# Four neighbouring tokens in a partition: another order of tokens inside a chunk of 512

## The chip, the cores and the metric

The kernel runs on one core of a Trainium2 chip. The metric is the device time of one execution in microseconds; the time of a version is the median over its runs. The trace was recorded by the hardware profiler in one further execution.

## What is computed

The reference is a two-layer network over x of shape (8, 128, 16, 16): 8 images, 128 channels, 256 places, so 2048 tokens of 128 channels. Each layer adds an attention block and then a mixture of experts to x. Cut to what matters here:

```python
x = x + _L0_conv_ref(_ln_c(x), ...)                   # linear attention with 5x5 depthwise convolutions
t = _to_tokens(x)                                     # (8, 256, 128)
t = t + _L0_ffn_ref(_ln_t(t), gate_w, w1, b1, w2, b2) # 8 experts, the best 2 of each token, gelu
x = _from_tokens(t, x)
x = x + _L1_conv_ref(_ln_c(x), wq, ..., bo)           # softmax attention over the 256 places of an image
t = _to_tokens(x)
t = t + _L1_ffn_ref(_ln_t(t), router_w, gate_w, up_w, down_w)  # 16 experts, the best 2, silu(gate) * up
```

In both mixtures a token's two best experts by router logit are taken, a softmax over those two logits gives their weights, and the token gets the weighted sum of the two experts' outputs.

## The kernel before

x lies in SBUF as `xs`, 128 channels in the partitions and 2048 tokens along the row, in 4 chunks of 512 tokens (`CH = 512`, `NCH = 4`). Five engines each run a program of their own; the order on each is written out by hand, and semaphores join them. SP and ACT each issue DMAs on a queue of their own, and POOL issues the indirect ones.

A mixture of experts (r = 0 and r = 1) runs in these steps:

1. **Rows.** `token_rows` on TensorE multiplies, for each of 16 tiles of 128 tokens, the tile of `xs` (the stationary operand) by a matrix that removes the mean over channels and gives the router logits. The result has tokens in the partitions. ScalarE scales it (L665) into `ln_sq`, and SP stores the rows, one DMA for a chunk, to `tok_dram[r]` in DRAM (`rows_store`, L395). Tile t of a chunk holds its tokens 128t to 128t + 127, one in each partition, so the store moves runs of 512 bytes.
2. **Router.** `router` on VectorE picks two experts for each token and works out, with TensorE's `slots`, a place for each of the 4096 pairs (token, choice) in a list ordered by expert. `pair_id` holds the number of the token that stands in each partition and tile, and from it come the lists `token` and `dest` (L969, L970).
3. **Gathers.** POOL fetches 32 blocks of 128 rows from `tok_dram` by `token` (L510), after all four stores have landed and `token` is ready.
4. **Experts.** For 39 (r = 0) or 47 (r = 1) items TensorE turns a block, multiplies it by the expert's weights (L1342, L1359), with ScalarE and VectorE in between; the sums go to `y_acc`.
5. **Scatters.** POOL writes the 32 blocks of outputs to `y_dram[r]` by `dest` (L517): first choices in the upper 2048 rows, second choices in the lower.
6. **Loaded back.** `y_load` waits until all scatters have landed and then issues four DMAs of 256 KB on SP's queue (first choices, into `xc`) and four on ACT's queue (second choices, into `ln_sq`), L364, each again in runs of 512 bytes. Chunk c is ready when both of its DMAs have landed (`y_in[c]`).
7. **Sum.** For each of 16 tiles ScalarE weighs the first choice (L711, `weigh_first`) and VectorE adds the weighed second one (L1056, `moe_sum`). After the four tiles of a chunk TensorE turns them into one PSUM bank (L1369, `y_columns`), and VectorE adds the bank to the chunk of `xs` (L1060). On VectorE the four adds of chunk c stand ahead of the L1060 of chunk c - 1.

What follows the sum of r = 0 is the layer norm of the second layer: TensorE's L1122 of chunk c - 1 stands behind the turns of chunk c, and its L1127 behind all of these. What follows the sum of r = 1 is the store of each chunk to `out` (L435).

Of the kernel before, what the change touches and what calls it, by code (L numbers as in the profile page):

```python
# [34 lines left out]
ALU = mybir.AluOpType  # L35
# [3 lines left out]
C = 128  # L39
B, HW = 8, 16  # L40
S = HW * HW
T = B * S
CH = 512
NCH = T // CH
TT = T // 128
# [21 lines left out]
E0, F0 = 8, 512  # L67
E1, F1 = 16, 256
# [37 lines left out]
def metaformer(nc, x, x_tok, qkv_w, taps_in, late_w, w1, w2, b2, up1, down1, out):  # L106


    tok_dram = [nc.dram_tensor(f"tok{r}", (T, C), F32, kind="Internal").ap() for r in range(2)]
# [3 lines left out]
    with ctx:  # L113
        def sb(name, shape, dt=F32, own=ctx):
            return own.enter_context(nc.sbuf_tensor(name, shape, dt))

        def sem(name):
            return ctx.enter_context(nc.semaphore(name))

        bank = [ctx.enter_context(nc.psum_tensor(f"bank{i}", [128, CH], F32)) for i in range(8)]  # L120
# [11 lines left out]
        pair_id = sb("pair_id", [128, 2, TT], F16)  # L132
        tok_w = sb("tok_w", [128, 2, C + E1])
# [21 lines left out]
        xs = sb("xs", [128, T])  # L155
# [117 lines left out]
        y_in = [sem(f"y_in{c}") for c in range(NCH)]  # L273
# [31 lines left out]
        def conv_send(queue, u, i, part=0, parts=1):  # L305

            t, v = UNITS[u]
            n = G8 // parts
            a = G8 * (v * GU + i) + n * part
            queue.dma_start(heads_agg[t][a:a + n, :, :, :].rearrange("p x y b -> p x (y b)"),  # L310
                            conv_out[n * part * HW:n * (part + 1) * HW, u % 2, i, :]).then_inc(conv_sent[u % 2], 16)
# [37 lines left out]
        def row_tile(r, i):  # L349

            n = C + (E0, E1)[r]
            return bank[ROW_BANKS[r][i // 3]][:, (i % 3) * n:(i % 3 + 1) * n]
# [3 lines left out]
        def chunk(t, c, n=CH):  # L356
            return t[:, c * n:(c + 1) * n]


        def y_load(queue, r, k):  # L360

            queue.wait_ge(moe[r].scattered, 16 * NB)
            for c in range(NCH):
                queue.dma_start(chunk((xc, ln_sq)[k], c).rearrange("p (t c) -> p t c", c=C),  # L364
                                y_dram[r][k * T + c * CH:k * T + (c + 1) * CH, :]
                                .rearrange("(t p) c -> p t c", p=128)).then_inc(y_in[c], 16)

        @block.sync
        def _(sp):
            def x_load(c):  # L370

                sp.dma_start(chunk(xs, c), chunk(x, c)).then_inc(x_in[c], 16)

            def xt_load(c):

                sp.dma_start(chunk(xc, c), chunk(x_tok, c)).then_inc(xt_in[c], 16)

            xt_load(0)
            xt_load(1)
            x_load(0)  # L380
            xt_load(2)
            x_load(1)
            xt_load(3)
            x_load(2)
            x_load(3)
            for i, (a, b) in enumerate(TAP_PARTS):
                sp.dma_start(taps[:, a:b, :], taps_in[:, a:b, :]).then_inc(taps_landed[i], 16)
                if i == 2:
                    sp.dma_start(wT[:, W_P0:W_SM + 1, :], late_w).then_inc(w_in, 16)

            def rows_store(r):

                for c in range(NCH):
                    sp.wait_ge(rows_copied, TT * r + 4 * c + 4)
                    sp.dma_start(tok_dram[r][c * CH:(c + 1) * CH, :].rearrange("(t p) c -> p t c", p=128),  # L395
                                 chunk(ln_sq, c).rearrange("p (t c) -> p t c", c=C)).then_inc(rows_out[r], 16)

            for n in range(len(UNITS) + MAPS_AHEAD):
                if n < len(UNITS):
                    t, v = UNITS[n]  # L400
                    sp.wait_ge(head_a, NCH * (n // UPT + 1))
                    for g in range(v * GU, (v + 1) * GU):
                        sp.dma_start(cmap[:, t, g, :],
                                     heads_raw[t][G8 * g:G8 * (g + 1), :, :, :].rearrange("p x y b -> p x (y b)"))\
                            .then_inc(map_in[n], 16)
                if n >= MAPS_AHEAD:
                    u = n - MAPS_AHEAD
                    if u < LAST:
                        sp.wait_ge(conv_copied, u + 1)
                        for i in (1, 3):  # L410
                            conv_send(sp, u, i)
            for i in range(GU):
                sp.wait_ge(conv_copied, LAST + 1 + i)
                conv_send(sp, LAST, i, 0, 2 if i == GU - 1 else 1)
            sp.wait_ge(conv_mm, LAST + GU)
            for i in range(2):
                sp.wait_ge(conv_sent[i], CONV_SENT[i])
            sp.dma_start(w_up0[:, :], w1).then_inc(moe_w[0], 16)
            sp.dma_start(w_down0[:, :], w2).then_inc(moe_w[0], 16)
            sp.wait_ge(x1_ready, NCH)  # L420
            sp.dma_start(b2_all[:, :], b2.rearrange("(a e) f -> a (e f)", a=1).broadcast_to([128, E0 * C]))\
                .then_inc(moe_w[0], 16)
            rows_store(0)

            for i in range(W1_LOADS):
                sp.wait_ge(moe[0].turned, 4 * i + 4)
                for w, src, n in ((w_up1, up1, 2 * F1), (w_down1, down1, 2 * C)):
                    cols = slice(i * E1 // W1_LOADS * n, (i + 1) * E1 // W1_LOADS * n)
                    sp.dma_start(w[:, cols], src[:, cols]).then_inc(moe_w[1], 16)
            y_load(sp, 0, 0)  # L430
            rows_store(1)
            y_load(sp, 1, 0)
            for c in range(NCH):
                sp.wait_ge(x_moe, NCH + c + 1)
                sp.dma_start(chunk(out, c), chunk(xs, c)).then_inc(stored, 16)  # L435
            sp.wait_ge(stored, 16 * NCH)
# [4 lines left out]
        def _(pool):  # L441
# [29 lines left out]
            def table(out, pattern, base, step):  # L471
                pool.iota(out, pattern, base=base, channel_multiplier=step,
                          allow_small_or_imprecise_dtypes=True).then_inc(tables, 1)
            table(low_high[:, 0, :], [[0, 2 * TT]], 127, 0)
            table(low_high[:, 1, :], [[0, 2 * TT]], (NB - 1) * 128, 0)
            table(pair_id[:, 0, :], [[128, TT]], 0, 1)
            table(pair_id[:, 1, :], [[128, TT]], -T, 1)
            table(col_id[:, :], [[0, 1]], 0, 1)
            table(item_id[:, :], [[1, NI1]], 0, 0)
            pool.memset(ones16[:, :], 1.0).then_inc(tables, 1)  # L480
# [276 lines left out]
        def _(dve):  # L757
# [118 lines left out]
            for n in range(B + 6):  # L876
                if n >= 7 and n % 2 == 1:
                    c = (n - 7) // 2
# [170 lines left out]
            def moe_sum(r):  # L1049

                dve.wait_ge(rt_weights, r + 1)
                for c in range(NCH + 1):
                    for i in range(4 * c, min(4 * c + 4, TT)):
                        rows = slice(i * 128, (i + 1) * 128)
                        dve.wait_ge(y_weighed, TT * r + i + 1)
                        dve.scalar_tensor_tensor(out=xc[:, rows], in0=ln_sq[:, rows], scalar=pair_w[:, 1, i:i + 1],  # L1056
                                                 in1=xc[:, rows], op0=ALU.mult, op1=ALU.add).then_inc(y_added, 1)
                    if c >= 1:
                        dve.wait_ge(y_turned, NCH * r + c)
                        dve.tensor_tensor(chunk(xs, c - 1), chunk(xs, c - 1), bank[c - 1][:, :], ALU.add)\  # L1060
                            .then_inc(x_moe, 1)

            router(0, E0)
# [9 lines left out]
            for i in range(B + 6):  # L1073
# [20 lines left out]
                if i >= 7 and i % 2 == 1:  # L1094
                    c = (i - 7) // 2
# [10 lines left out]
        def _(pe):  # L1106
# [114 lines left out]
            for s in range(GU * len(UNITS)):  # L1221
# [18 lines left out]
                u, i = s // GU, s % GU  # L1240
                t, v = UNITS[u]
# [8 lines left out]
                for k in (2, 1, 3, 0, 4):  # L1250
                    y0, y1 = max(0, EDGE - k), min(HW, HW + EDGE - k)
                    mm = pe.matmul(bank[b][:, i * 128 + y0 * B:i * 128 + y1 * B], cw[:, u % CWR, i, k, :],  # L1252
                                   cmap[:, t, v * GU + i, (y0 + k - EDGE) * B:(y1 + k - EDGE) * B],
                                   start=(k == EDGE), stop=(k == 4))
# [10 lines left out]
            def token_rows(r, g):  # L1265

                pe.wait_ge((x1_ready, x3_ready)[r], ROW_GROUPS[g][-1] // 4 + 1)
                for i in ROW_GROUPS[g]:
                    mm = pe.matmul(row_tile(r, i), xs[:, i * 128:(i + 1) * 128], tok_w[:, r, 0:C + (E0, E1)[r]],  # L1269
                                   start=True, stop=True)  # L1270
                mm.then_inc(rows_mm, 1)

            pe.wait_ge(router_out, 3)
            for n in range(B + 4):
# [6 lines left out]
                if n >= 5 and n % 2 == 1:  # L1281
                    c = (n - 5) // 2
# [104 lines left out]
            for g in range(4):  # L1387
                for j in range(4):
                    i = 4 * g + j
                    mm = pe.matmul(bank[V_BANKS[g]][:, j * 128:(j + 1) * 128], xn[:, i * 128:(i + 1) * 128],  # L1390
                                   wT[:, W_AV, :], start=True, stop=True)
# [36 lines left out]
            for i in range(B + 5):  # L1428
# [6 lines left out]
                if i >= 6 and i % 2 == 0:  # L1435
                    c = (i - 6) // 2
# [70 lines left out]
```

## Time and profile before

| what | value |
|---|---|
| median of 3 runs | 446.07 us (444.70 to 447.37) |
| the profiled execution's own time | 447.75 us |
| its span, first to last instruction | 446.0 us |
| PE busy / weight loads / DVE / ACT / POOL | 79% / 68% / 50% / 47% / 40% of the span |
| mean granted clock of TensorE | 0.892 of full speed |
| DMA | 38.47 MB in 34184 packets, 28640 of them under 2 KB |

The busy shares are means over stages with different limits. TensorE is busiest, and over the whole span the chain that ended last lies 63% on PE, 8% on DMA and 8% on DVE. Between the last scatter and the last sum of each layer TensorE has nothing to do but the turns, so those two stretches, some 13 us each, are read by themselves.

### The profile page before, as it was taken

Reading aid. Unit: us, or ns where it says so; the run is one execution under the profiler, and the core shown is the slowest. Engines: PE = TensorE matmul, PEld = TensorE weight load, DVE = VectorE, ACT = ScalarE, POOL = GpSimd, SP = SyncE. Lnnn points to the kernel's source line nnn. Section 1 sums busy time; section 2 is a strip of 40 time slices with the busy share of each in tenths; the row PEclk is TensorE's granted clock in tenths of the full one; section 3 lists DMA queues with packets and bytes.
Section 4 is the critical chain, followed back from the end, with each engine's and each line's share of the span. In section 5 each row is a group of like instructions: output and inputs, shape, how many; then the busy total and the mean of one; then the engine's idle time right before and its main releaser. Section 6 shows DMA issues by size and latency. Waiting matters only on the chain.

```text
span 446.0 us, 7931 instructions
## 1 busy us (share of the span) xinstructions
PE 352.9 (79%) x2404; PEld 301.4 (68%) x2404; DVE 222.9 (50%) x565; ACT 210.9 (47%) x554; POOL 178.0 (40%) x202
## 2 busy tenths in 40 slices
PE   3889999997956598957999399898267988977813
PEld 1359999985734598957998265776246888877802
DVE  3618555513675156534776373776841343444306
ACT  4651333333574256734663364566533565554304
POOL 3819554400033655573556000003066555555530
PEclk9999999999896679995999789999665999999875
DMA  7444444324822546310111700000311111111146
GB/s 239 202 74 99 102 96 83 48 37 70 343 73 88 194 176 239 124 49 30 37 38 43 194 2 0 1 1 0 96 42 41 43 43 37 44 36 37 35 119 194
DMA packets 34184, 38.47 MB, mean 86 GB/s; under 512 B 3680, under 2 KB 28640, under 8 KB 33376
## 3 DMA queue, kind: packets, MB, share of 16 engines
q1 hardware_dynamic: 22620, 25.79, 19.8%
q0 software_dynamic: 4096, 8.40, 6.0%
q10 hardware_dynamic: 7428, 3.77, 3.9%
q8 instruction: 22, 0.36, 0.3%
q14 instruction: 18, 0.15, 0.1%
HBM read 24.31 MB, written 7.34 MB: 71 GB/s over the span
## 4 chain that ended last, share of the span: by engine, by line
PE 63%; DMA 8%; DVE 8%; ACT 6%; issue 6%; another core or an unknown queue 5%; ACTq 1%; POOL 1%; SPq 1%; POOLq 0%; DVEq 0%
PE bank L1342 18%; PE bank L1359 12%; PE bank L1252 10%; DMA ln_sq<-y 2%; PE bank L1204 2%; PE bank L1351 2%; PE bank L1424 2%; PE bank L1269 2%; PE bank L1189 2%; ACT w_block L684 2%; PE bank L1383 2%; POOL y L517 1%; PE bank L1133 1%; DMA x_rows<-tok,token 1%
## 5 line engine op out<-in xcount | busy, mean ns | idle before, releaser
L1342 PE MATMUL bank<-x_cols,w_block 128*128 x688 | 104.0, 300 | 20.5 <-ACT w_block L684 9.7
L1342 PEld LDWEIGHTS bank<-x_cols,w_block 128*128 128x128 f32 x688 | 94.1, 212 | 24.5 <-issue 24.3
L510 POOL DMA_INDIRECT x_rows<-tok,token x64 | 60.6, 947 | 65.2 <-DVE dest L970 26.9
L517 POOL DMA_INDIRECT y<-wide,dest x64 | 62.1, 970 | 49.4 <-DVE wide L1046 39.6
L1359 PE MATMUL bank<-w_down,h_cols 128*128 x500 | 75.4, 290 | 4.8 <-DVE wide L1046 3.2
L1359 PEld LDWEIGHTS bank<-w_down,h_cols 128*128 128x128 f32 x500 | 66.9, 203 | 7.3 <-issue 7.0
L1252 PE MATMUL bank<-cmap,cw 128*128 128x112 f32 (+2 forms) x480 | 57.4, 275 | 1.9 <-DMA cmap<-heads 1.9
L1252 PEld LDWEIGHTS bank<-cmap,cw 128*128 128x128 f32 x480 | 55.7, 192 | 3.7 <-DMA cmap<-heads 2.7
L684 ACT ACTIVATE w_block<-w_up 128x512 f32 x86 | 53.6, 623 | 0.9 <-issue 0.9
L321 POOL TENSOR_TENSOR cw<-taps 128x640 f32<-128x640 f32 x24 | 35.7, 1514 | 36.7 <-PE bank L1252 29.5
L1029 DVE TENSOR_TENSOR h_cols<-h_in,bank 128x256 f32<-128x256 f32 x47 | 19.8, 421 | 53.4 <-ACT h_in L701 32.0
L504 POOL MEMSET wide<- 128x4096 f32 x2 | 7.0, 3512 | 98.3 <-DVE xs L1097 60.7
L687 ACT ACTIVATE x_cols<-bank 128x128 f32<-128x128 f32 x64 | 16.3, 275 | 50.8 <-PE bank L1351 29.6
L1021 DVE TENSOR_TENSOR h_in<-bank,wT 128x512 f32<-128x512 f32 x39 | 26.9, 691 | 24.2 <-remote 13.0
L695 ACT ACTIVATE h_cols<-h_in 128x512 f32<-128x512 f32 x39 | 24.5, 629 | 22.7 <-DVE h_in L1021 19.3
L701 ACT ACTIVATE h_in<-bank 128x256 f32<-128x256 f32 x47 | 17.9, 383 | 20.2 <-PE bank L1342 16.7
L1351 PE MATMUL bank<-ident,x_rows 128*128 128x128 f32 x64 | 18.1, 308 | 9.5 <-ACT x_cols L687 5.1
L321 DVE TENSOR_TENSOR cw<-taps 128x640 f32<-128x640 f32 x24 | 23.7, 1020 | 2.2 <-PE bank L1252 2.2
L1369 PE MATMUL bank<-ident,wide 128*128 128x128 f32 x32 | 8.1, 403 | 19.8 <-DVE wide L1056 19.8
L711 ACT ACTIVATE wide<-wide,pair_w 128x128 f32<-128x128 f32 x32 | 10.2, 390 | 26.2 <-DMA ln_sq<-y 26.2
L1369 PEld LDWEIGHTS bank<-ident,wide 128*128 128x128 f32 x32 | 5.6, 205 | 24.1 <-DVE wide L1056 23.2
L1046 DVE SCALAR_TENSOR_TENSOR wide<-bank,item,wide 128x128 f32 x47 | 16.3, 347 | 8.2 <-PE bank L1359 6.6
(188 smaller groups left out, 524.8 us busy)
## 6 DMA issues: line engine op xcount, KB each, us to landing
w_up<-in_up_dram SPq DMA_DIRECT2D x4, 1024.0 KB
cmap<-heads SPq DMA_DIRECT2D x48, 64.0 KB
w_up<-in_w_dram SPq DMA_DIRECT2D x1, 2048.0 KB, 7.7
w_down<-in_w_dram SPq DMA_DIRECT2D x1, 2048.0 KB, 13.7
tok<-ln_sq SPq DMA_DIRECT2D x8, 256.0 KB, 2.4
w_down<-in_down_dram SPq DMA_DIRECT2D x4, 512.0 KB
wide<-y SPq DMA_DIRECT2D x8, 256.0 KB, 5.6
ln_sq<-y ACTq DMA_DIRECT2D x8, 256.0 KB, 6.1
```

The costliest lines, as they stand in the source:

```text
L321: engine.tensor_tensor(cw[:, u % CWR, i, :, :].rearrange("p k (o x) -> p k o x", x=HW), taps[:, g, KS * HW:TAP].unsqueeze(1).unsqueeze(3). ...
L510: pool.indirect_dma_start(out=x_rows[:, j % RING, :], out_offset=None, in_=tok_dram[r], in_offset=bass.IndirectOffsetOnAxis(ap=token[r][:, ...
L517: pool.indirect_dma_start(out=y_dram[r], in_=y_acc[:, s * C:(s + 1) * C], in_offset=None, out_offset=bass.IndirectOffsetOnAxis(ap=dest[r][ ...
L684: act.activation(w_block[:, n % 3, :], (w_up0, w_up1)[r][:, bass.ds(e * F0, F0)], ACT.Copy).then_inc(m.w, 1)
L695: act.activation(h_cols[:, j % HBUF, :], h_in[:, j % HBUF, :], ACT.Gelu_apprx_tanh)\
L701: act.activation(h_in[:, j % HBUF, 0:F1], bank[2 + j % UPS][:, 0:F1], ACT.Silu)\
L1021: dve.tensor_tensor(h_in[:, j % HBUF, :].rearrange("p (k s) -> p k s", k=M0), bank[2 + j % UPS][:, :].rearrange("p (k s) -> p k s", k=M0), ...
L1029: dve.tensor_tensor(h_cols[:, j % HBUF, 0:F1], h_in[:, j % HBUF, 0:F1], bank[2 + j % UPS][:, F1:2 * F1], ALU.mult).then_inc(m.h_in, 1)
L1252: mm = pe.matmul(bank[b][:, i * 128 + y0 * B:i * 128 + y1 * B], cw[:, u % CWR, i, k, :], cmap[:, t, v * GU + i, (y0 + k - EDGE) * B:(y1 + ...
L1342: mm = pe.matmul(bank[2 + j % UPS][:, i * 128:(i + 1) * 128], w_block[:, j % 3, i * 128:(i + 1) * 128], x_cols[:, bass.ds(place[j] & ((NB ...
L1351: pe.transpose(bank[k % 2][:, 0:128], x_rows[:, k % RING, :], ident[:, :]).then_inc(m.turned, 1)
L1359: mm = pe.matmul(bank[6 + j % 2][:, 0:C], h_cols[:, j % HBUF, i * 128:(i + 1) * 128], w_down[:, bass.ds(ej * (K * C) + i * C, C)], start=( ...
```

## The change

Inside a chunk, partition p now holds tokens 4p to 4p + 3 of the chunk, and tile j of the chunk holds the tokens 4p + j. Five places follow from this:

- `rows_store` and `y_load` describe the DRAM side as `(p t)` in place of `(t p)`: a partition's four rows are neighbours in DRAM, one run of 2 KB.
- `pair_id` is filled by the new numbering (two iota instructions, as before, of another pattern).
- `token_rows` takes the stationary operand through `tokens_of`: every fourth token of a chunk, a step of 16 bytes in place of neighbouring words.
- The L1060 add reads the turned bank in the order of the tokens: four words 512 bytes apart, then the next four. Its other operand and its output stay contiguous.

Counts and sizes of instructions, of DMAs and of their bytes stay the same. Which rows of a block stand in which order changes.

```diff
+        def tokens_of(t, i):
+            return chunk(t, i // 4).rearrange("p (q j) -> p j q", j=4)[:, i % 4, :]
...
                 queue.dma_start(chunk((xc, ln_sq)[k], c).rearrange("p (t c) -> p t c", c=C),
                                 y_dram[r][k * T + c * CH:k * T + (c + 1) * CH, :]
-                                .rearrange("(t p) c -> p t c", p=128)).then_inc(y_in[c], 16)
+                                .rearrange("(p t) c -> p t c", p=128)).then_inc(y_in[c], 16)
...
-                    sp.dma_start(tok_dram[r][c * CH:(c + 1) * CH, :].rearrange("(t p) c -> p t c", p=128),
+                    sp.dma_start(tok_dram[r][c * CH:(c + 1) * CH, :].rearrange("(p t) c -> p t c", p=128),
                                  chunk(ln_sq, c).rearrange("p (t c) -> p t c", c=C)).then_inc(rows_out[r], 16)
...
-            table(pair_id[:, 0, :], [[128, TT]], 0, 1)
-            table(pair_id[:, 1, :], [[128, TT]], -T, 1)
+            table(pair_id[:, 0, :].rearrange("p (c j) -> p c j", c=NCH), [[CH, NCH], [1, 4]], 0, 4)
+            table(pair_id[:, 1, :].rearrange("p (c j) -> p c j", c=NCH), [[CH, NCH], [1, 4]], -T, 4)
...
-                        dve.tensor_tensor(chunk(xs, c - 1), chunk(xs, c - 1), bank[c - 1][:, :], ALU.add)\
+                        xs_c = chunk(xs, c - 1).rearrange("p (q j) -> p q j", j=4)
+                        dve.tensor_tensor(xs_c, xs_c, bank[c - 1][:, :].rearrange("p (j q) -> p q j", j=4), ALU.add)\
                             .then_inc(x_moe, 1)
...
-                    mm = pe.matmul(row_tile(r, i), xs[:, i * 128:(i + 1) * 128], tok_w[:, r, 0:C + (E0, E1)[r]],
+                    mm = pe.matmul(row_tile(r, i), tokens_of(xs, i), tok_w[:, r, 0:C + (E0, E1)[r]],
                                    start=True, stop=True)
```

## Rows read from the trace of the kernel before

**Rows 1.** The chain that ended last, r = 0: start, length, what
```profile
139.34 2.50 DMA x_rows<-tok,token
...
247.54 5.57 DMA ln_sq<-y
...
254.84 1.12 PE bank L1369 x4
...
259.16 0.44 PE bank L1369 x4
```

**Rows 2.** The same chain, sum of r = 1
```profile
436.08 0.41 ACT wide L711
...
437.75 0.60 DVE xs L1060
438.35 1.20 DVE wide L1056 x4
...
441.33 1.13 PE bank L1369 x4
...
442.49 0.69 DVE xs L1060
```

**Rows 3.** Timeline of both sums: start, length, engine, line [idle before, releaser]
```profile
247.05 2.14 ACTq L364 DMA_DIRECT2D ln_sq<-y  x4
251.38 1.28 ACT L711 ACTIVATE wide<-wide,pair_w 128x128 f32<-128x128 f32 x4 [11.01 <-DMA ln_sq<-y]
...
258.33 0.69 DVE L1060 TENSOR_TENSOR xs<-xs,bank 128x512 f32<-128x512 f32 x1
...
430.15 2.13 ACTq L364 DMA_DIRECT2D ln_sq<-y  x4
434.33 1.28 ACT L711 ACTIVATE wide<-wide,pair_w 128x128 f32<-128x128 f32 x4 [12.25 <-DMA ln_sq<-y]
434.83 1.16 DVE L1056 SCALAR_TENSOR_TENSOR wide<-ln_sq,pair_w,wide 128x128 f32<-128x128 f32 x4 [9.05 <-ACT wide L711]
...
436.52 1.23 DVE L1056 SCALAR_TENSOR_TENSOR wide<-ln_sq,pair_w,wide 128x128 f32<-128x128 f32 x4 [0.53 <-ACT wide L711]
```

**Rows 4.** Timeline and DMA issues of the rows' store
```profile
131.72 3.45 SPq L395 DMA_DIRECT2D tok<-ln_sq  x4
...
tok<-ln_sq SPq DMA_DIRECT2D x8, 256.0 KB, 2.4
```

**Rows 5.** Windows; the last two columns are DMA share and GB/s
```profile
250.50:255.50 5.00, 1.77 (x7) 1.37 (x8) 3.10 (x10) 3.12 (x10) 0.00 (x0) 0.56 1.16 291
...
7.00:8.00 1.00, 0.00 (x0) 0.00 (x0) 0.27 (x3) 0.76 (x3) 0.00 (x0) 1.00 1.03 387
...
7.00:9.50 2.50, 0.41 (x1) 0.41 (x2) 1.59 (x12) 2.01 (x8) 0.00 (x0) 1.00 0.97 327
```

**Rows 6.** Timeline of the start, and DMA issues: KB each, us to landing
```profile
0.80 0.87 SPq L376 DMA_DIRECT2D wide<-in_x_tok_dram  x2
4.91 0.87 DVE L785 BATCH_NORM_STATS2 x_stat<-wide 128x6 f32<-128x128 f32 x4 [4.91 <-DMA wide<-in_x_tok_dram]
...
b_all<-in_b_dram SPq DMA_DIRECT2D x1, 512.0 KB, 3.6
```

**Rows 7.** Groups by line and shape: busy us, mean ns | idle before
```profile
L1060 DVE TENSOR_TENSOR xs<-xs,bank 128x512 f32<-128x512 f32 x8 | 5.5, 683 | 1.2 <-PE bank L1369 1.2
L947 DVE TENSOR_REDUCE slot_i<-hots 128x32 int32<-128x512 f32 x1 | 1.0, 1011 | 0.0
L554 ACT ACTIVATE heads<-bank 128x512 f32<-128x512 f32 x12 | 11.9, 1093 | 5.9 <-PE bank L1147 5.9
L539 ACT ACTIVATE ln_sq<-bank 128x512 f32<-128x512 f32 x4 | 2.3, 590 | 0.5 <-PE bank L1122 0.5
L1177 PEld LDWEIGHTS bank<-ident,heads 128*128 128x128 f32 x32 | 4.2, 188 | 0.0
L1269 PEld LDWEIGHTS bank<-tok_w,xs 128*128 128x128 f32 x64 | 8.2, 190 | 1.9 <-issue 1.2 <-DVE xs L1097 0.5 <-DVE xs L882 0.2
```

## The prediction

> **What bounds the kernel now.** I read three views. First the chain that ended last, for the places where the changed transfers stand on it. The reader is to see three kinds of them: the first gather (2.50 us at 139.34), the loading of y (5.57 us from 247.54), and, behind each load, the sum [rows 1, 2]. The store of rows is not there. Its four issues end at 131.72 + 3.45 = 135.17 us, the last lands at most 2.4 us later, at 137.57 [rows 4], and the first gather starts only at 139.34 [rows 1], when the list of tokens is ready. So a quicker store is worth nothing while it lands in those 1.8 us.
>
> Second, the timeline of the two sums. From the issue of y_load to ScalarE's first L711 it is 251.38 - 247.05 = 4.33 us in layer 0 and 434.33 - 430.15 = 4.18 us in layer 1 [rows 3]. Then VectorE adds chunk 0 in 1.16 us, sits idle 0.53 us until chunk 1 is loaded and weighed (0.52 us in layer 0), and from there on it is busy: L1056 x4 (1.23 to 1.15 us) and L1060 (0.60 us on the chain) take turns three times [rows 2, 3]. The transfer therefore sets two things alone: when chunk 0 lands, and that idle half microsecond. Behind it, in layer 1, two L1060 and the adds stand in a row on VectorE; then comes the last turn (1.13 us) and the last L1060 (0.69 us). The third L1060 runs beside that turn: from its start at 441.33 to the last L1060 at 442.49 it is 1.16 us, so 0.47 us are left beside the third one's 0.69 [rows 2]. In layer 0 TensorE is the longer one from 254.84 on, because L1122 stands between its turns (five pieces, L1369 and L1122 in alternation, to 259.60, of which the first and the last are shown) [rows 1]. VectorE's third L1060 ends there at 258.33 + 0.69 = 259.02, which is 0.58 us before the last turn ends at 259.60 [rows 1, 3].
>
> Third, the groups by line, for prices of strided reading [rows 7].
>
> **The change part by part.** Let a be what chunk 0 lands earlier, b what is left out of the idle 0.53 us, and d what one L1060 costs more.
>
> *a, per layer.* With runs of 512 bytes chunk 0 takes 4.33 and 4.18, mean 4.25 us. The nearest row with runs of 2 KB is the first load of the kernel: issued at 0.80, used at 4.91, 4.11 us [rows 6]. That gives a = 0.15. The bounds: zero, since the first transfers of both kinds ramp up for some two microseconds, and 4.25 - 3.6 = 0.65, from the one load of 512 KB in runs of 4 KB that had the queues to itself [rows 6]. I take 0.15, since that row has the runs of this change.
>
> *b, per layer.* In the steady part y moves at 291 GB/s, so the 512 KB of a chunk take 524288 / 291 = 1.80 us. Loads in runs of 2 KB move at 387 GB/s in their best microsecond and 327 GB/s over 2.5 us [rows 5]: 1.35 or 1.60 us. Chunk 1 can be added some 0.43 us after it lands (one L711 stands in the chain for 0.41 from 436.08, and the adds start at 436.52) and VectorE is free 1.66 us after chunk 0 landed (434.83 + 1.16 - 434.33) [rows 2, 3]. The idle time becomes 1.35 + 0.43 - 1.66 = 0.12 or 0.37 us. I take the middle, 0.25, so b = 0.28, between 0.16 and 0.41. Beyond that nothing more is gained: VectorE needs 1.83 us for a chunk (1.23 + 0.60), more than the load does. This is why a large part of the faster transfer goes nowhere. The Trainium skill (DMA: Bandwidth & Descriptors, Why small descriptors are slow) puts some 3 cycles on each packet beside one for every 32 bytes: 19 for 512 bytes, so 76 against 67 for 2 KB, an estimate of 1.80 x 67 / 76 = 1.59 us for a chunk. That is the slower of the two rows; by it b would be 0.16 and the sum below 0.24 us longer.
>
> *d.* L1060 takes 683 ns with a contiguous bank [rows 7]. No row shows VectorE reading PSUM with a step. The nearest is L947, which reads 512 words of SBUF 64 bytes apart in 1011 ns: 0.33 us more than 512 words in a row. Below that stands zero (PSUM may not mind). Above it stands ScalarE, which needs 1093 ns where it writes 512 words 512 bytes apart and 590 where they are neighbours: 0.50 us more [rows 7]. I take 0.33, as it is the same engine, the same number of words and a read. The Trainium skill (Advanced Engine Details and Errata, Memory Cachelines) says that a PSUM line holds 8 bytes, two words, and that every two consecutive elements should be neighbours for best throughput. It speaks against this read and gives no time, so it makes the sum no other; no run so far shows a strided PSUM read.
>
> Where d lands: in layer 1 two L1060 stand ahead of the last adds and one behind the last turn, so 3d; the third is covered by the 0.47 us. In layer 0 three of them first eat the 0.58 us by which TensorE is longer, the fourth stands in the open: 4d - 0.58, but no less than d. With d = 0.33: 0.99 and 0.74.
>
> *At nothing.* The stationary tile read with a step of 16 bytes: L1177 loads weights 32 bytes apart in 188 ns against 190 for today's L1269 [rows 7]; 26 of those stand in the open per layer, and no row gives a dearer price. The two iota run in the first microseconds, beside the first load that everything waits for [rows 6]. The store of rows is hidden as above; if it were not, it would cost what it lands after 139.34. The order of rows in gathers and scatters: the same number of 512-byte rows through the same instructions; only the first gather (2.50 us) stands bare, like the last scatter of each layer. A tenth of it more or less would be 0.25 us; I take zero.
>
> **The sum.** Layer 0: 0.74 - 0.28 - 0.15 = +0.31. Layer 1: 0.99 - 0.28 - 0.15 = +0.56. Together +0.87 us on the profiled execution: 447.75 + 0.9 = 448.6 us. That execution ran 1.68 us above the median of the runs, so the forecast for the median is 446.07 + 0.9 = 447.0 us, 0.2% more. About 0.5%, 2.2 us, is what a measurement of this kernel can tell from no change.
>
> **The rivals.**
> *PSUM read at no extra cost.* d = 0, and both layers gain a + b: -0.86 us, 445.2. For it speaks that the reads of PSUM and of SBUF need not be alike; against it that every strided access on both engines that the groups show has its price.
> *Early landing.* d = 0, a = 0.65 and b = 0.41: -2.12 us, 443.95, on the edge of what can be told. For it: 0.65 is a landing that this chip showed. Against it: that load had one queue's DMA alone, while here two queues start together, and the kernel's own first load in 2 KB runs took 4.11 us.
> *The strided add becomes the bound.* Place: L1060, eight times. From d = 0.47 on the third L1060 of layer 1 outgrows its cover too, and the loss is 4d - 0.58 and 4d - 0.47 less the 0.86 of a and b: above 2.2 us from d = 0.52 on, that is, when an L1060 takes 1.2 us. With d = 0.7 it is 2.22 + 2.33 - 0.86 = +3.7, 449.8. For it: ScalarE's strided write is nearly there. Against it: VectorE's own strided row is at 0.33.
> *The transfer is no faster.* a = b = 0 with d = 0.33: +1.73, 447.8. It would be so if the two halves of a chunk were held up by something other than the packets; the speeds of rows 5 speak against it.
>
> **How the numbers follow.** Forecast (d between 0.2 and 0.5) 0.45; free PSUM read 0.25; early landing 0.12; strided add as bound 0.11; no faster transfer 0.07. The bounds give 443.9 (early landing) and, with d = 0.50, a = 0 and b = 0.16, +2.6 us, 448.7; the range is 443.9 to 448.7. Faster by over 0.5%: most of early landing and a tail of the free read, in which a scatter or gather order also helps, 0.18. Slower: the strided bound and a part of the forecast's and the last rival's tails, 0.19. Within: 0.63.
>
> **What would show it.** The L1060 group: 1.0 us right, 0.68 or 1.2 us wrong. ScalarE's first L711 some 4.1 us after the issue; well under 3.9 means early landing. VectorE's idle time ahead of chunk 1's adds: 0.1 to 0.4 us. The store of rows lands before the list of tokens is ready, L1269's weight loads stay at 190 ns, the first gather at 2.3 to 2.5 us. A weight load of over 250 ns, a gather of 3 us, or a stretch of the experts that is longer or shorter would make the prediction wrong by a way that I have not priced.

## The result, and the profile after

| what | before | after |
|---|---|---|
| median, us (range; runs) | 446.61 (444.70 to 447.37; 4) | 452.71 (451.94 to 455.53; 4) |
| the profiled execution's own time, us | 447.75 | 455.53 |
| its span, us | 446.0 | 453.8 |
| mean granted clock of TensorE | 0.892 | 0.888 |
| DMA packets (under 2 KB) | 34184 (28640) | 24968 (16352) |

After stands to before as 1.0155, with a 95% interval of 1.0098 to 1.0211. The kernel became slower by 6.1 us by the medians and by 6.9 us by this ratio, and 452.71 us lies outside the predicted range, which ended at 448.7. The transfers did change as described: as many megabytes in 9216 packets fewer. The time was lost elsewhere.

The lines that the change adds shift those behind them: L364 is now L368, L1269 is now L1274, L1177 is L1182, L1369 is L1374, L1056 is L1060, L1060 is L1065, L711 is L715.

The first view to read is the groups by line and shape of the changed kernel: busy us, mean ns of one, then idle time before. Its rows answer to [rows 7].

```profile
L1274 PEld LDWEIGHTS bank<-tok_w,xs 128*128 128x128 f32 x64 | 15.5, 327 | 1.4 <-issue 0.5 <-DVE xs L886 0.2 <-DVE xs L1102 0.2
...
L1182 PEld LDWEIGHTS bank<-ident,heads 128*128 128x128 f32 x32 | 4.2, 189 | 0.0
...
L1065 DVE TENSOR_TENSOR xs<-xs,bank 128x512 f32<-128x512 f32 x8 | 5.5, 684 | 1.9 <-PE bank L1374 1.9
```

A weight load of `token_rows` takes 327 ns where it took 190. The group of L1182, which the prediction used as its price, stays at 189. The strided add, for which the prediction feared most, takes 684 ns against 683. (In these rows the operands behind the arrow are the moving one and then the stationary one: what L1182 loads is `heads`, every word of it 32 bytes from the next.)

The chain that ended last shows where the dearer load stands. First the kernel before, at two places not shown so far (start, length, what; x6 and x26 are passes of TensorE, two for each product of a tile):

```profile
120.60 0.69 PE bank L1269 x6
...
123.01 3.03 PE bank L1269 x26
...
304.04 0.73 PE bank L1269 x6
...
305.63 3.20 PE bank L1269 x26
...
324.91 2.32 DMA x_rows<-tok,token
```

Then the changed kernel, with the pieces that answer to [rows 1, 2]:

```profile
121.19 1.28 PE bank L1274 x6
...
124.18 5.96 PE bank L1274 x26
...
143.58 2.51 DMA x_rows<-tok,token
...
252.91 3.38 DMA ln_sq<-y
...
256.37 0.41 ACT wide L715
...
259.33 1.11 PE bank L1374 x4
...
264.21 0.44 PE bank L1374 x4
...
309.10 1.29 PE bank L1274 x6
...
311.25 5.97 PE bank L1274 x26
...
333.63 2.33 DMA x_rows<-tok,token
...
450.27 0.69 DVE xs L1065
```

The 26 passes take 5.96 us in place of 3.03, and 5.97 in place of 3.20. The six ahead of them nearly double too. Nothing hides this: the router waits for the logits that come with the rows. Between the first of these passes and the first gather lie 143.58 - 121.19 = 22.39 us, where it was 139.34 - 120.60 = 18.74, and in layer 1 it is 333.63 - 309.10 = 24.53 against 324.91 - 304.04 = 20.87. That is 3.65 and 3.66 us more, 7.3 together.

The third view is the timeline of both sums, which answers to [rows 3]:

```profile
252.91 1.80 ACTq L368 DMA_DIRECT2D ln_sq<-y  x4
256.37 2.52 ACT L715 ACTIVATE wide<-wide,pair_w 128x128 f32<-128x128 f32 x8 [10.29 <-DMA ln_sq<-y]
256.88 2.40 DVE L1060 SCALAR_TENSOR_TENSOR wide<-ln_sq,pair_w,wide 128x128 f32<-128x128 f32 x8 [6.51 <-ACT wide L715]
...
438.74 1.80 ACTq L368 DMA_DIRECT2D ln_sq<-y  x4
442.31 1.28 ACT L715 ACTIVATE wide<-wide,pair_w 128x128 f32<-128x128 f32 x4 [11.66 <-DMA ln_sq<-y]
...
444.54 1.23 DVE L1060 SCALAR_TENSOR_TENSOR wide<-ln_sq,pair_w,wide 128x128 f32<-128x128 f32 x4 [0.56 <-ACT wide L715]
445.68 0.68 DVE L1065 TENSOR_TENSOR xs<-xs,bank 128x512 f32<-128x512 f32 x1
```

From the issue to ScalarE's first L715 it is 256.37 - 252.91 = 3.46 us and 442.31 - 438.74 = 3.57 us, against 4.33 and 4.18. So the longer runs give back 0.87 and 0.61 us. In layer 0 the adds of two chunks now follow each other without a gap (eight in 2.40 us); in layer 1 the gap ahead of chunk 1 is still there, 0.56 us. The windows of the loading of y (the last three columns are TensorE's granted clock, DMA share and GB/s) and the DMA issues of the page say the same of the transfers:

```profile
255.00:259.50 4.50, 1.28 (x5) 0.89 (x6) 2.61 (x9) 2.66 (x9) 0.00 (x0) 0.69 1.04 390
...
124.18:130.14 5.96, 5.96 (x28) 5.96 (x27) 1.57 (x6) 3.85 (x27) 3.51 (x1) 1.00 0.27 89
```

```profile
tok<-ln_sq SPq DMA_DIRECT2D x8, 256.0 KB, 2.0
```

y moves at 390 GB/s, not 291 [rows 5]. Over the same 4.5 us of the kernel before, 249.14 to 253.64 us, which take in its start, it is 303. The store lands after 2.0 us in place of 2.4 and is still hidden: the list of tokens comes later than it. The second window lies over the 26 dear passes: the granted clock there is 1.00, the upper of the two levels, 2.4 GHz, as it is over the 26 passes of the kernel before. So the clock is not what makes them dear.

The stages add up: +7.31 us from rows to first gather, -1.48 for the loading of y, -0.14 for the sums (worked out below), together +5.7. The two profiled spans differ by 7.8. The other 2.1 lie ahead of the first rows (+0.6) and in the experts of layer 0, from first gather to y_load: 252.91 - 143.58 = 109.33 us against 247.05 - 139.34 = 107.71, +1.6. The 0.6 mean little: in the traces of the experiments that leave everything ahead of the rows as it was, the first rows begin between 119.65 and 122.90 us. The 1.6 are taken up with the experiments.

### The profile page after: what moved, and what is told of

The parts are those of the page before. It is cut to its first block, busy times and chain, and to the rows that moved or that the text cites. A ratio compares the mean times of both kernels' runs of the same rounds, so it can differ in the third digit from the quotient of the medians.

```text
span 453.8 us, 7931 instructions
## 1 busy us (share of the span) xinstructions
PE 364.4 (80%) x2404; PEld 310.8 (69%) x2404; DVE 221.7 (49%) x565; ACT 212.2 (47%) x554; POOL 178.1 (39%) x202
## 2 busy tenths in 40 slices
DMA packets 24968, 38.47 MB, mean 85 GB/s; under 512 B 3680, under 2 KB 16352, under 8 KB 24160
## 4 chain that ended last, share of the span: by engine, by line
PE 66%; DVE 8%; DMA 7%; ACT 6%; issue 5%; another core or an unknown queue 4%; POOL 1%; ACTq 1%; SPq 1%; DVEq 0%; POOLq 0%
PE bank L1347 18%; PE bank L1257 12%; PE bank L1364 11%; PE bank L1274 3%; PE bank L1356 2%; ACT w_block L688 2%; DMA ln_sq<-y 2%; PE bank L1429 2%; PE bank L1388 2%; PE bank L1194 2%; PE bank L1209 1%; DMA wide<-in_x_tok_dram 1%; POOL y L521 1%; DVE wide L1060 1%
## 5 line engine op out<-in xcount | busy, mean ns | idle before, releaser
L1347 PE MATMUL bank<-x_cols,w_block 128*128 x688 | 105.9, 303 | 20.5 <-ACT w_block L688 15.0
L1347 PEld LDWEIGHTS bank<-x_cols,w_block 128*128 128x128 f32 x688 | 95.5, 215 | 25.7 <-issue 25.5
L1257 PE MATMUL bank<-cmap,cw 128*128 128x112 f32 (+2 forms) x480 | 59.0, 279 | 1.9 <-DMA cmap<-heads 1.9
L1257 PEld LDWEIGHTS bank<-cmap,cw 128*128 128x128 f32 x480 | 57.3, 197 | 3.7 <-DMA cmap<-heads 2.8
L1374 PE MATMUL bank<-ident,wide 128*128 128x128 f32 x32 | 8.4, 412 | 17.8 <-DVE wide L1060 17.7
L715 ACT ACTIVATE wide<-wide,pair_w 128x128 f32<-128x128 f32 x32 | 10.2, 390 | 23.1 <-DMA ln_sq<-y 22.9
L1374 PEld LDWEIGHTS bank<-ident,wide 128*128 128x128 f32 x32 | 5.7, 209 | 22.3 <-DVE wide L1060 20.9
L1045 DVE TENSOR_TENSOR y_part<-bank,b_all 128x128 f32<-128x128 f32 x39 | 11.3, 290 | 17.7 <-PE bank L1364 7.6
```

Of the source, the lines that this page charges most:

```text
L1347: mm = pe.matmul(bank[2 + j % UPS][:, i * 128:(i + 1) * 128], w_block[:, j % 3, i * 128:(i + 1) * 128], x_cols[:, bass.ds(place[j] & ((NB ...
```

## The experiments

Two theories stood at the start: that the loss is the stationary operand's step and all else is gain or nothing, or that a good part comes from the order of rows, the numbering or the strided add.

### The parts one by one

**e2_step16** is the kernel before with the strided stationary operand alone:

```diff
-  mm = pe.matmul(row_tile(r, i), xs[:, i * 128:(i + 1) * 128], tok_w[:, r, 0:C + (E0, E1)[r]],
+  mm = pe.matmul(row_tile(r, i), tokens_of(xs, i), tok_w[:, r, 0:C + (E0, E1)[r]],
```

> The kernel before, with the stationary tile of token_rows alone read with a step of 16 bytes (tokens come into other partitions, and nothing else follows them, so the output is of permuted tokens). Theory 1: weight loads 327 ns, 26 passes in 6.0 us in each layer, 6 us more than before, ratio 1.013 (1.010 to 1.016). Theory 2: the weight loads are slow but less than half of the 6 us is theirs, ratio under 1.007.

Measured: 454.56 us (4 runs) against 446.10, ratio 1.0180 (1.0128 to 1.0232). The groups by line and shape of e2_step16:

```profile
L1273 PEld LDWEIGHTS bank<-tok_w,xs 128*128 128x128 f32 x64 | 15.5, 327 | 1.4 <-issue 0.5 <-DVE xs L886 0.2 <-DVE xs L1101 0.2
```

This one edit has the whole loss and somewhat more: the same 327 ns, the same 5.96 and 5.97 us for the 26 passes, and 22.38 and 24.46 us from rows to first gather. Its ratio lies above the 1.010 to 1.016 written down: rows to first gather make 7.2 us of some 8. In its trace the experts of layer 0 are 1.6 us longer, as in the changed kernel.

**e1_labels** is the opposite: all of the change but the two strided accesses. A row number in DRAM is only a label there: tile j of a chunk still holds tokens 128j to 128j + 127, but partition p's four rows are neighbours in DRAM, and `pair_id` holds row numbers by that rule. Gathers, scatters, store and y_load agree on the label, and nobody else reads it.

```diff
 # as in the change: (p t) in y_load and rows_store, and the new pair_id; the two lines below stay as before
   mm = pe.matmul(row_tile(r, i), xs[:, i * 128:(i + 1) * 128], ...
   dve.tensor_tensor(chunk(xs, c - 1), chunk(xs, c - 1), bank[c - 1][:, :], ALU.add)
```

> The 2 KB runs and the new numbers in pair_id are kept, the tile of xs that TensorE loads and the add of the turned bank are as before: a partition's four rows get neighbouring row numbers in DRAM, and no engine reads with a step. Theory 1 (the loss is the stationary operand read with a step of 16 bytes): weight loads of token_rows back at 190 ns, the 26 passes ahead of the router back at 3.0 us from 6.0, ScalarE's first L711 some 3.5 us after the issue as in the changed kernel, so about 1.6 us less than before, ratio 0.996 (0.993 to 0.999). Theory 2 (part of the loss comes from the order of rows in gathers and scatters, or from the longer runs: the profiled execution of the changed kernel was 1.6 us longer in the experts of layer 0): this kernel keeps both and stays 1 us or more above before, ratio over 1.002.

Measured: 445.01 us (12 runs) against 446.10 (23 runs), ratio 0.9957 (0.9928 to 0.9986). The chain of e1_labels:

```profile
123.72 3.03 PE bank L1273 x26
...
247.86 3.38 DMA ln_sq<-y
...
251.33 0.41 ACT wide L715
...
254.28 1.11 PE bank L1373 x4
...
258.66 0.44 PE bank L1373 x4
```

The rows cost 3.03 us again. From the issue of y_load to the first L715 it is 251.33 - 247.86 = 3.47 us, and 3.62 in layer 1: the gain of the changed kernel without its loss. The experts of layer 0 take 107.74 us. This version beats both kernels. The gain is small: 1.9 us by the ratio, 1.1 us by the medians. Its interval excludes no change, but half a per cent lies within it.

**e3_add** is the kernel before with the strided read of the PSUM bank alone:

```diff
-  dve.tensor_tensor(chunk(xs, c - 1), chunk(xs, c - 1), bank[c - 1][:, :], ALU.add)
+  xs_c = chunk(xs, c - 1).rearrange("p (q j) -> p q j", j=4)
+  dve.tensor_tensor(xs_c, xs_c, bank[c - 1][:, :].rearrange("p (j q) -> p q j", j=4), ALU.add)
```

> The kernel before, with the add of the turned bank alone reading PSUM 512 bytes apart (its columns land in permuted places of xs, so the output differs). If the read of PSUM is free, as the 0.68 us in the changed kernel's trace say: the add stays at 680 ns and the ratio within 0.997 to 1.003. If it costs what VectorE's strided read of SBUF costs: 1010 ns, and 1.7 us more.

Measured: 445.79 us (10 runs), ratio 1.0003 (0.9966 to 1.0040). The group of the strided add in e3_add:

```profile
L1061 DVE TENSOR_TENSOR xs<-xs,bank 128x512 f32<-128x512 f32 x8 | 5.5, 682 | 2.7 <-PE bank L1370 2.7
```

682 ns strided, 683 contiguous: no price at all.

**e11_cont_add** is the changed kernel with the contiguous add put back, everything else kept:

```diff
-  xs_c = chunk(xs, c - 1).rearrange("p (q j) -> p q j", j=4)
-  dve.tensor_tensor(xs_c, xs_c, bank[c - 1][:, :].rearrange("p (j q) -> p q j", j=4), ALU.add)
+  dve.tensor_tensor(chunk(xs, c - 1), chunk(xs, c - 1), bank[c - 1][:, :], ALU.add)
```

> The changed kernel with the add of the turned bank contiguous as before (its columns land in permuted places of xs, so the output differs). The add took 0.68 us in both ways, so this is the same as the changed kernel: some 6.5 us over before, ratio 1.010 to 1.021, L1269's successor at 327 ns, load to first use 3.5 us. If the strided add has a part in the loss, it is 1 us or more below that.

Measured: 452.61 us (4 runs), ratio 1.0072 (1.0044 to 1.0099), less than was expected. Its own time is that of the changed kernel, 452.71; what was different is the kernel before, which took 449.21 us beside these runs (8 of them), and 446.10 to 446.98 beside the others. In its trace the rows take 22.30 and 24.38 us to the first gather, as in the changed kernel, and the sums 8.87 and 8.41 us from first weighing to last add (9.01 and 8.65 there). By its ratio alone the strided add could have some 3 us of the loss. The traces speak against that: the add takes the same 0.68 us in both ways, the sums are only 0.14 and 0.24 us shorter without the step, and e3_add shows no loss. Why the kernel before took longer beside these runs was not found.

**e9_layer1** and **e10_layer0** are e2_step16 in one layer only:

```diff
+  mm = pe.matmul(row_tile(r, i), (tokens_of(xs, i) if r == 1 else xs[:, i * 128:(i + 1) * 128]), ...   # e9_layer1
+  mm = pe.matmul(row_tile(r, i), (tokens_of(xs, i) if r == 0 else xs[:, i * 128:(i + 1) * 128]), ...   # e10_layer0
```

> The kernel before, with the strided stationary tile in layer 1 alone (tokens permuted in that layer's output). Open is what made the experts of layer 0 take 109.3 us (first gather to loading of y) in all three kernels with strided loads and 106.2 to 107.7 in the six others. If the strided loads of layer 0 lead to it: under 108 us here, with layer 1 alone 3.6 us longer from its rows to its first gather (24.7 us, 21.0 in layer 0's kernel before). If it came by chance: 109.3 can show here too.

> The kernel before, with the strided stationary tile in layer 0 alone (tokens permuted in that layer). If the strided loads of layer 0 lead to the longer experts: 109.3 us again, and rows to first gather 22.5 us in layer 0 and 21.0 in layer 1. If by chance: any value between 106 and 109.5.

Measured, one run each beside the same runs of the kernel before as e11_cont_add: 453.68 and 452.70 us against 449.21. From rows to first gather e9_layer1 takes 18.84 us in layer 0 and 24.48 in layer 1, e10_layer0 22.40 and 21.17. Each layer pays its own 3.6 us (18.74 and 20.87 before), and the other 0.1 and 0.3. The experts of layer 0 take 106.61 us in e9_layer1 and 106.54 in e10_layer0, although the latter has the same strided loads ahead of them as the changed kernel. The 1.6 us that this stage had more in the profiles of the changed kernel, e2_step16 and e4_step32 (109.33, 109.31, 109.31) therefore do not follow from the dear loads alone. Without them the stage lay between 106.2 and 107.8 in all traces; e11_cont_add with them had 107.68.

TensorE's granted clock tells where the 1.6 us lie. In the 5.5 us that begin 34 us behind the first gather it is 0.69 in those three traces, and TensorE runs 28 matmuls there; in every other trace, e10_layer0 and e11_cont_add among them, it is 1.00, with 49 to 52 matmuls. The timeline of the changed kernel shows what came before it:

```profile
175.82 1.15 PE L1364 MATMUL bank<-w_down,h_cols 128*128 x8 [0.77 <-DVE wide L1050]
178.31 2.07 PE L1347 MATMUL bank<-x_cols,w_block 128*128 x8 [1.34 <-ACT w_block L688]
```

TensorE stood idle twice, for a sum on VectorE and for a copy of weights on ScalarE, and the eight matmuls behind the second wait took 2.07 us at the lower level of 1.2 GHz. It is the same in e2_step16 and e4_step32 (0.82 and 1.34 us). In the kernel before, e10_layer0 and e11_cont_add it stood idle there once, for 1.25, 1.13 and 1.25 us, and the next eight took 1.15. Why the wait for the sum came in three of the five traces with dear loads in layer 0 stays open.

### Why the load is dear

**e5_step8** and **e4_step32** put other steps into the kernel before: tiles of every second token (8 bytes) and of every eighth (32 bytes, for which a group of rows waits for two chunks of `xs`). The lines are what `tokens_of` returns to `token_rows`:

```diff
+  chunk(t, i // 4).rearrange("p (q j) -> p j q", j=2)[:, i % 4 // 2, i % 2 * 128:i % 2 * 128 + 128]   # e5_step8
+  chunk(t, i // 8, 2 * CH).rearrange("p (q j) -> p j q", j=8)[:, i % 8, :]                            # e4_step32
```

> The kernel before, the stationary tile of token_rows read with a step of 8 bytes: every second token of 256 (tokens of the output permuted). If what counts is whether the words are neighbours: weight loads 325 to 335 ns as with 16 and 32 bytes. If it counts how many words lie in 16 bytes: between 190 and 330 ns, or 190.

> As the one with 16 bytes, with a step of 32 bytes (tokens of a stretch of 1024, so the rows of a tile wait for both chunks; the output is of permuted tokens). Theory A, a transpose loads differently from a product: weight loads stay near 330 ns here, though the transposes L1177 read 32 bytes apart in 188. Theory B, the step of 16 bytes is a bad one and 32 is not: 190 ns. Theory C, the price grows with the step: over 400 ns.

Measured, one run each: e5_step8 443.94 us against 446.98, e4_step32 456.04 against 446.10. The group of the weight loads in e5_step8:

```profile
L1273 PEld LDWEIGHTS bank<-tok_w,xs 128*128 128x128 f32 x64 | 8.3, 196 | 1.9 <-issue 1.2 <-DVE xs L1101 0.5 <-DVE xs L886 0.2
```

and in e4_step32:

```profile
L1273 PEld LDWEIGHTS bank<-tok_w,xs 128*128 128x128 f32 x64 | 15.9, 334 | 1.4 <-issue 0.5 <-DVE xs L1101 0.3 <-DVE xs L886 0.2
```

Steps of 4, 8, 16 and 32 bytes cost 190, 196, 327 and 334 ns, and the 26 passes on the chain 3.03, 3.07, 5.96 and 6.11 us: a threshold between 8 and 16, not a price that grows with the step. The Trainium skill (Advanced Engine Details and Errata, Memory Cachelines) says that SBUF is read in lines of 16 bytes and that two hits in a line are needed to hide its latency. These four numbers agree: a step of 8 leaves two words in each line, a step of 16 one, and so does a step of 32. The prediction had drawn on the PSUM lines of the same section and passed over this one.

**e6_twice** asks whether 3 us more of TensorE work ahead of the router delays the kernel by just that, whatever makes the work. It issues each product of `token_rows` twice, contiguous:

```diff
-  for i in ROW_GROUPS[g]:
+  for i in [i for i in ROW_GROUPS[g] for _ in range(2)]:
```

> The kernel before, with every product of token_rows issued twice, contiguous (same output). It delays the router by about the 3 us that the strided loads cost, with TensorE at full speed. The kernels with strided loads all took 109.3 us from the first gather of layer 0 to the loading of y, the others 106.7 to 107.7. Theory S (the strided loads themselves leave TensorE at its lower clock for longer): 107.7 us here, 26 passes become 52 in some 6.1 us, total some 6.5 us over before. Theory D (any such delay does it, by where the stretches of low clock fall): 109.3 us here, and 8 us over before.

Measured: 455.21 us (4 runs) against 446.98, ratio 1.0178 (1.0106 to 1.0250). Its chain:

```profile
120.75 1.39 PE bank L1269 x12
...
123.85 6.04 PE bank L1269 x52
...
143.32 2.75 DMA x_rows<-tok,token
```

52 passes at the old price take 6.04 us, as 26 dear ones take 5.96, and from rows to first gather it is 143.32 - 120.75 = 22.57 us. The time of the kernel is that of e2_step16. So the place is fully open, and a stride costs there what doing the work twice costs. The delays here, 3.83 us in layer 0 and 4.08 in layer 1, are higher than the 3 us written down beforehand, which had counted the 26 passes and left out the group ahead of them (1.39 us in place of 0.69). Of the two theories each had half: the experts of layer 0 take 106.21 us, not 109.3, so a delay of this size does not lengthen them by itself; but the whole is 8.2 us over before, not 6.5.

**e7_kv_product** turns to the row from which the price had been read. L1177 reads its stationary operand with a step of 32 bytes, but it is a transpose. Here it becomes a product of the same operand with the identity:

```diff
-  mm = pe.transpose(bank[2 + i % 2][:, j * 128:(j + 1) * 128],
-                    kv[:, (j % 2) * 8:(j % 2) * 8 + 8, :, b], ident[:, :])
+  mm = pe.matmul(bank[2 + i % 2][:, j * 128:(j + 1) * 128],
+                 kv[:, (j % 2) * 8:(j % 2) * 8 + 8, :, b], ident[:, :], start=True, stop=True)
```

> The kernel before, with the turns L1177 of the linear attention written as products with the identity in place of transposes: the same stationary operand, 32 bytes apart, which loads in 188 ns in a transpose. If a transpose is what made that row cheap: two passes for each, and weight loads of 325 to 335 ns. If the address pattern was: 190 ns.

Measured: 470.04 us in one run, 23 more. Two groups of e7_kv_product:

```profile
L1177 PEld LDWEIGHTS bank<-ident,heads 128*128 128x128 f32 x64 | 15.9, 333 | 0.0
...
L1189 PEld LDWEIGHTS bank<-kvT 128*128 128x128 f32 x64 | 8.7, 195 | 0.0
```

The same operand, step and line cost 188 ns as a transpose and 333 ns as a product, twice for each (x64 in place of x32). `heads` is the loaded operand in both. The products of L1189 behind it load at 195. But 188 ns is not a transpose without a price. In the kernel before, another transpose reads its operand without a step, at a granted clock of 1.00 like L1177:

```profile
L1413 PEld LDWEIGHTS bank<-ident,sq_pn 128*128 128x128 f32 x32 | 3.8, 141 | 3.3 <-DVE sq_pn L1087 2.4 <-issue 0.5
```

**e8_turn16** is the cross-check: L1369, a transpose, gets a step of 16 bytes in the kernel before.

```diff
-  xc[:, (4 * c + i) * 128:(4 * c + i + 1) * 128], ident[:, :])
+  tokens_of(xc, 4 * c + i), ident[:, :])
```

> The kernel before, with the turns L1369 reading every fourth column (16 bytes apart; output permuted). If transposes are free of the price: weight loads 205 ns as before, sum stretch 8.9 us in both layers. If the price is that of any strided load: over 330 ns.

Measured: 448.92 us in one run. The group of e8_turn16:

```profile
L1373 PEld LDWEIGHTS bank<-ident,wide 128*128 128x128 f32 x32 | 5.8, 215 | 23.6 <-DVE wide L1060 22.7 <-issue 0.8
```

Contiguous, the mean of this group is 205 ns in the kernel before, and 204 to 219 over the other traces, so 215 tells nothing: most of these turns run at the lower level of the clock, and the mean mixes both levels. The last turns of layer 0 run at a granted clock of 1.00 in both kernels. The timeline of the weight loads there, first the kernel before, then e8_turn16:

```profile
258.57 0.14 PEld L1369 LDWEIGHTS bank<-ident,wide 128*128 128x128 f32 x1 [0.24 <-DVE wide L1056]
```

```profile
258.85 0.20 PEld L1373 LDWEIGHTS bank<-ident,wide 128*128 128x128 f32 x1 [0.24 <-DVE wide L1060]
```

The shortest load of the group is 141 ns before and 195 here. So a transpose does pay for the step, 141 to 195 ns at 16 bytes and to 188 at 32, but less than a product, and little of it reaches the chain: the last four turns of layer 0 take 0.47 us in place of 0.44. From the first weighing to the last add the sums take 8.97 and 9.03 us (8.94 and 8.85 before). Why transposes pay so much less was not found.

## Why the prediction was wrong

**The step that failed** is the first under "At nothing": "The stationary tile read with a step of 16 bytes: L1177 loads weights 32 bytes apart in 188 ns against 190 for today's L1269". The two numbers are right, but they set a transpose with a step beside a product without one. Against its own kind the row already showed a price, 188 ns against the 141 of L1413, and the loads that it was to price are those of products: 333 ns for that very operand in a product (e7_kv_product), 327 at 16 bytes (e2_step16). "No row gives a dearer price" was true and no bound. An edit on a bare stretch got a single value from a row of another kind of instruction, and no rival. All 32 passes of a layer stand in the open, not 26. On the chain they take 2.93 + 0.59 = 3.52 us more in layer 0 and 2.77 + 0.56 = 3.33 in layer 1, and the first gathers come 3.65 and 3.66 us later against their rows. (137 ns more for each of 32 loads would be 4.4 us. Loads overlap: 64 of 327 ns make 20.9 us, and the group was busy for 15.5.) The prediction had named the sign by which it would fall: "A weight load of over 250 ns".

**a was too small.** 0.15 us for each layer was taken, between 0 and 0.65; measured 0.87 and 0.61. One trace on each side gives these two. Over all traces the landing takes 4.23 to 4.44 us in layer 0 and 3.94 to 4.22 in layer 1 with runs of 512 bytes, and 3.46 to 3.67 and 3.56 to 3.62 with 2 KB. The nearest row with runs of 2 KB, the first load of the kernel, had taken 4.11 us for one DMA of 256 KB, while a chunk of y is two; why it took longer no run tells. The bound from the load in runs of 4 KB was passed in layer 0. Four issues on ACT's queue also take 1.80 us in place of 2.14 [rows 3].

**b was too small, and the clock took part of it back.** 0.28 us for each layer was taken. In layer 0 the gap on VectorE is gone, and the whole of it is gained up to the turn of chunk 1: from the first weighing to that turn it is 259.33 - 256.37 = 2.96 us against 254.84 - 251.38 = 3.46. From there to the end of the last turn, where TensorE is the longer one as the prediction had found, it takes 264.65 - 259.33 = 5.32 us against 259.60 - 254.84 = 4.76. The granted clock over these two stretches is 0.60 and 0.68: both begin at the lower level, and the upper one comes back between 263.33 and 263.83 us in the changed kernel and between 257.84 and 258.34 in the kernel before, which is some 1 us sooner in its stretch. So layer 0 ends 0.06 us worse, by a clock that no part of the prediction holds. That is one execution: in e1_labels the same two stretches take 2.95 and 4.82 us, at a clock of 0.67 in the second. In layer 1 the gap stays at 0.56, but to the end of the last add it is 450.96 - 442.31 = 8.65 us against 443.18 - 434.33 = 8.85, so 0.20 is gained. Together 0.14. In e1_labels it is 0.45 and 0.41, with no gap in either layer.

**d was too large.** 0.33 us was taken from a reduction that reads SBUF with a step; it is nothing for this add (684 and 682 ns against 683). Whether the memory or the operation makes the difference no run tells. The rival of the free PSUM read was right in this, and what the prediction cites on PSUM lines does not show in this add.

**Right** were the hidden store (2.0 us to landing), the gathers' order (2.51 and 2.33 us for the first gathers, 2.50 and 2.32 before) and the place of each transfer on the chain.

Put together with the measured terms, the change without the strided operand would have been -0.87 - 0.61 - 0.14 = -1.6 us. That is nearest to the rival "early landing" (-2.12 us), which e1_labels bears out: its trace gains 0.86 + 0.56 in the landings and 0.45 + 0.41 in the sums, 2.3 us, its ratio says 1.9 us and its medians 1.1. So the forecast's own sum, +0.87 us, had the wrong sign too, by a and d. With 7.31 us for the strided operand the sum is +5.7 us; the medians differ by 6.1.

## What to carry to other kernels

When an edit puts a step into an operand on the path that sets the end, price it by a row with the same kind of instruction, the same operand slot and the same memory; where no row has all three, give it bounds from both sides and a rival, even if the nearest row says nothing. Ask of each number whether the row beside it differs in one thing alone: 188 against 190 ns differed in two, the step and the kind of instruction, and they cancelled. Here the passes of an fp32 product cost no more while two words of the stationary operand lay in 16 bytes, and twice as much with one. And look for what must really move: longer runs in DRAM needed only another numbering of rows, and the tokens could stay where the engines read them in a row.

## What the runs showed of the hardware

- A weight load of an fp32 product takes 190, 196, 327 and 334 ns at steps of 4, 8, 16 and 32 bytes; one of an fp32 transpose takes 141 ns without a step, 195 at 16 bytes and 188 at 32, all at a granted clock of 1.00. On the chain 26 passes of products go from 3.03 to 5.96 us at 16 bytes, four transposes from 0.44 to 0.47.
- VectorE's add of 512 fp32 words from PSUM takes as long with a step of 512 bytes as without (682 and 683 ns), while the reduction from SBUF with a step of 64 bytes took 1011 [rows 7]; the two differ in the operation too.
- Two queues loading together reached 390 GB/s over 4.5 us in runs of 2 KB, against 291 in runs of 512 bytes [rows 5] (303 over the 4.5 us of the kernel before that answer to these), and the first chunk was ready 0.6 to 0.9 us earlier.
